# Window attention's key and query norms: an inverse root by a power on GpSimd in place of ScalarE's logarithm and exponential and VectorE's Newton step

## What is computed

```python
qkv = shift_token(x) @ wqkv                 # q, k, v: 8 heads of 64
q, k = l2norm(q) * q_scale, l2norm(k) * k_scale     # l2norm(t) = t / max(norm(t), 1e-12)
q, k = rotary_xpos(q, k)
sim  = 8 * q @ k.T                          # window of 128 and the one before it, masked
o    = softmax(sim) @ v
x    = x + o @ wo
h    = layernorm(shift_token(x)) @ w1 + b1  # a, g = halves of it
x    = x + (a * gelu(g)) @ w2 + b2
```

## Time and profile before

| | us |
|---|---|
| median of three runs (lowest, highest) | 1368.27 (1363.14, 1372.32) |
| the profiled execution, its own time | 1366.47 |
| its span, first to last instruction | 1364.7 |
| busy: TensorE (PE), VectorE (DVE) | 1241.3, 970.3 |
| busy: ScalarE (ACT), GpSimd (POOL) | 923.6, 634.0 |
| granted TensorE clock, mean over the span | 0.968 |

### The profile page before, as it was taken

One profiled execution on the slowest core, in us unless ns is written; L12 is line 12 of the kernel. 1 busy time (PEld: TensorE's weight loads), 2 busy tenths in 40 slices (PEclk: granted clock), 3 DMA queues, 4 the chain that ended last, 5 costly groups with the idle time before them and its releaser, 6 DMA issues.

```text
span 1364.7 us, 26379 instructions
## 1 busy us (share of the span) xinstructions
PE 1241.3 (91%) x9057; PEld 1061.2 (78%) x9057; DVE 970.3 (71%) x2602; ACT 923.6 (68%) x2023; POOL 634.0 (46%) x697
## 2 busy tenths in 40 slices
PE   2799999999999993899966988999999999999986
PEld 2699889989988993677754657888888887888886
DVE  5767666666767646998776787678788778777532
ACT  2455765565576552888936769778778788888643
POOL 6523521452353214444333556556656657655433
PEclk9799999999999997999987999999999999999999
DMA  7300010010000004000010001100100000000010
GB/s 165 103 1 14 32 32 1 14 64 0 1 1 1 1 0 114 1 17 17 9 65 1 1 5 52 40 5 5 46 4 4 20 5 13 20 21 21 21 31 17
DMA packets 34881, 33.75 MB, mean 25 GB/s; under 512 B 11340, under 2 KB 31424, under 8 KB 34752
## 3 DMA queue, kind: packets, MB, share of 16 engines
q1 hardware_dynamic: 33856, 29.91, 7.1%
q0 software_dynamic: 768, 2.10, 0.9%
q10 hardware_dynamic: 128, 0.04, 0.0%
HBM read 25.75 MB, written 4.19 MB: 22 GB/s over the span
## 4 chain that ended last, share of the span: by engine, by line
PE 40%; ACT 8%; DVE 4%; issue 3%; POOL 3%; DMA 2%; SPq 1%; ACTq 0%; DVEq 0%; POOLq 0%
PE w_ring L1633 2%; PE w_ps_p L1663 2%; PE w_ring L1635 2%; PE w_ring L1634 2%; PE w_ring L1713 2%; PE a_ps L845 2%; PE w_ring L1714 2%; PE w_ring L1715 2%; PE w_ps_a L1681 2%; PE w_ring L1640 2%; DMA w_xs<-X 2%; PE w_ring L1725 2%; PE w_ps_d L1656 1%; PE w_ps_d L1653 1%; PE w_ring L1726 1%
## 5 line engine op out<-in xcount | busy, mean ns | idle before, releaser
L360 ACT ACTIVATE t_gf<-t_ps_f,t_fb_cur 128x512 f32<-128x512 f32 x128 | 87.9, 686 | 165.8 <-PE t_ps_f L280 164.2
L508 DVE TENSOR_TENSOR t_g_lo<-t_gf,t_g_hi 128x512 fp32r<-128x512 f32 x128 | 92.1, 721 | 81.5 <-ACT t_g_hi L362 80.5
L293 PE MATMUL t_ps_o<-t_w_hi,t_g_hi 128*128 128x256 f32 x512 | 145.8, 285 | 1.1 <-DVE t_g_lo L508 1.1
L295 PE MATMUL t_ps_o<-t_w_hi,t_g_lo 128*128 128x256 f32 x512 | 144.8, 283 | 0.0
L294 PE MATMUL t_ps_o<-t_w_lo,t_g_hi 128*128 128x256 f32 x512 | 144.8, 283 | 0.0
L1713 PE MATMUL w_ring<-w_nh,w_w_hi 128*128 128x256 f32 x384 | 113.3, 295 | 12.8 <-DVE w_gate L2241 6.2
L644 POOL TENSOR_TENSOR t_rs<-t_ve,t_neghalf 128x4 f32<-128x4 f32 x32 | 38.2, 1194 | 178.7 <-DVE t_ve L469 177.2
L2196 DVE COPY w_pt<-w_ps_p 128x384 f32<-128x384 f32 x128 | 70.5, 550 | 60.7 <-PE w_ps_p L1663 59.6
L278 PE MATMUL t_ps_f<-t_nh,t_w_hi 128*128 128x512 f32 x256 | 103.5, 404 | 6.9 <-DVE t_nl L607 3.6
L1714 PE MATMUL w_ring<-w_nh,w_w_lo 128*128 128x256 f32 x384 | 108.0, 281 | 0.0
L1715 PE MATMUL w_ring<-w_nl,w_w_hi 128*128 128x256 f32 x384 | 107.9, 281 | 0.0
(11 more groups left out here) (290 smaller groups left out, 4368.6 us busy)
## 6 DMA issues: line engine op xcount, KB each, us to landing
t_raw<-in_L_tok_w SPq DMA_DIRECT2D x8, 1024.0 KB
out<-X SPq DMA_DIRECT2D x14, 256.0 KB, 2.2
raw<-in_L_ffn_wqkv SPq DMA_DIRECT2D x2, 1536.0 KB, 6.8
raw<-in_L_ffn_w SPq DMA_DIRECT2D x4, 682.0 KB, 5.2
w_raw_o<-out SPq DMA_DIRECT2D x8, 256.0 KB, 3.0
w_xs<-X SPq DMA_DIRECT2D x16, 127.0 KB
w_raw<-in_L_ffn_w SPq DMA_DIRECT2D x2, 640.0 KB
t_raw_d<-in_L_tok_D SPq DMA_DIRECT2D x4, 256.0 KB
```

The lines of the kernel that those rows point to most:

```text
L293: pe.matmul(out, g_hi[:, j % 4, tok], w2_hi[:, j, :], start=(j == 0 and t % 2 == 0), stop=False, skip_group_check=True)
L295: mm = pe.matmul(out, g_lo[:, j % 4, tok], w2_hi[:, j, :], start=False, stop=(j == FC - 1 and t % 2 == 1), skip_group_check=True)
L360: act.activation(gf[:, j % 2, :], ps_f[:, j % 2, :], ACT.Gelu, bias=fb_cur[:, j:j + 1]).then_inc(pf_free, 1)
L508: dve.tensor_tensor(g_lo[:, j % 4, :], gf[:, j % 2, :], g_hi[:, j % 4, :].bitcast(F32), ALU.subtract).then_inc(g_split, 1)
```

## The change

ScalarE's `root` and VectorE's `inverse_root` are taken out with their calls, and so are their four tiles and four semaphores. GpSimd's `scale_k` now begins with one power: `rn = sc ** -0.5` on the tile of 128 x 2 x 8, after a wait for the clamp and, from the third unit on, for the softmax steps that read the older `rn` of the same place (VectorE had this wait before). A tile `nhalf` of the same size, holding -0.5, is set once by VectorE in `pads`.

```diff
--- before.py
+++ after.py
@@ -1378,12 +1378,9 @@
     al = sb("al", [P, DC, STOK], F32R)
     ss = sb("ss", [P, 2, H])
     sc = sb("sc", [P, ST, 2, H])
-    lg = sb("lg", [P, ST, 2, H])
-    y0 = sb("y0", [P, ST, 2, H])
-    ya = sb("ya", [P, ST, 2, H])
-    yb = sb("yb", [P, ST, 2, H])
+    nhalf = sb("nhalf", [P, 2, H])
     rn = sb("rn", [P, 2, ST, 2, H])
-    return raw_o, raw_2, ln_all, b1_all, b2_all, tab, neghalf, ident, mask, x0_st, x0_mv, x0_ve, x0_rs, xs, ah, al, ss, sc, lg, y0, ya, yb, rn
+    return raw_o, raw_2, ln_all, b1_all, b2_all, tab, neghalf, ident, mask, x0_st, x0_mv, x0_ve, x0_rs, xs, ah, al, ss, sc, nhalf, rn
 
 
 def window_phase(nc, sems, X, dram, out, raw, qkv, opening, done):
@@ -1422,7 +1419,7 @@
 
         raw_qkv = raw[:, :].rearrange("p (c n) -> p c n", c=DC)
         raw_1 = raw[:, :].rearrange("p (c u n) -> p c u n", c=DC, u=2)
-        raw_o, raw_2, ln_all, b1_all, b2_all, tab, neghalf, ident, mask, x0_st, x0_mv, x0_ve, x0_rs, xs, ah, al, ss, sc, lg, y0, ya, yb, rn = opening
+        raw_o, raw_2, ln_all, b1_all, b2_all, tab, neghalf, ident, mask, x0_st, x0_mv, x0_ve, x0_rs, xs, ah, al, ss, sc, nhalf, rn = opening
         scl = raw_2[:, 0:2, :].rearrange("p c n -> p (c n)").rearrange("p (i u x) -> p i u x", i=2, u=2)
         m1 = sb("m1", [P, ST, 2, INNER])
         m2 = sb("m2", [P, 2, INNER])
@@ -1466,7 +1463,7 @@
 
         names = ("h_out h_in_0 h_in_1 b2_added stored vec ident maskz mask pad padp fill raw_qkv raw_o raw_2 raw_1 hi_qkv hi_o hi_2 hi_1 "
                  "split_qkv split_o split_2 split_1 tab x0 x0_st x0_mv x0_ve x0_rs t1_full ah_done split1 q_full k_full v_full sq_0 sq_1 "
-                 "ss_0 ss_1 q_read k_read rota_0 rota_1 sc_done lg_done y0_done ya_done yb_done rn_done kscaled qs_full ks_full qt_done kt_done v_done "
+                 "ss_0 ss_1 q_read k_read rota_0 rota_1 sc_done rn_done kscaled qs_full ks_full qt_done kt_done v_done "
                  "d_full sm_done p_done ri scaled p_full pt_done pv_done ot_h ot_split y_full x_mid shifted_0 shifted_1 st mv ve rs nmr xn "
                  "t2_full nf_done split2 g_full gelu_done a_full gated h_hi h_split h_used xb x_out")
         S = {x: sem(x) for x in names.split()}
@@ -1941,13 +1938,6 @@
                     act.wait_ge(done["v_full"], 2 * NSQ)
                 act.activation(m2[:, i, :], ring[:, RB[b], :], ACT.Square).then_inc(S[f"sq_{i}"], 1)
 
-            def root(n, t):
-
-                act.wait_ge(S["sc_done"], 2 * n + t + 1)
-                act.activation(lg[:, t, :, :], sc[:, t, :, :], ACT.Ln).then_inc(S["lg_done"], 1)
-                act.wait_ge(S["lg_done"], 2 * n + t + 1)
-                act.activation(y0[:, t, :, :], lg[:, t, :, :], ACT.Exp, scale=-0.5).then_inc(S["y0_done"], 1)
-
             def turned(n, t, i, b):
                 act.wait_ge(S["ks_full" if i else "qs_full"], 2 * n + t + 1)
                 if n >= 2:
@@ -2059,8 +2049,6 @@
                 if real(c):
                     probabilities(H * c + 0)
                     probabilities(H * c + 1)
-                if real(b):
-                    root(b, 0)
                 if real(c):
                     probabilities(H * c + 2)
                     probabilities(H * c + 3)
@@ -2075,8 +2063,6 @@
                     hi_1(1, 1)
                 if h == 13:
                     hi_2(1)
-                if real(b):
-                    root(b, 1)
                 if h == 3:
                     hi_o(0)
                 if real(c):
@@ -2160,18 +2146,6 @@
                     dve.wait_ge(S[f"ss_{i}"], 2 * n + t + 1)
                 dve.tensor_scalar(sc[:, t, :, :], ss[:, :, :], 1e-24, None, ALU.max).then_inc(S["sc_done"], 1)
 
-            def inverse_root(n, t):
-
-                k = 2 * n + t
-                dve.wait_ge(S["y0_done"], k + 1)
-                dve.tensor_tensor(ya[:, t, :, :], y0[:, t, :, :], y0[:, t, :, :], ALU.mult).then_inc(S["ya_done"], 1)
-                dve.wait_ge(S["ya_done"], k + 1)
-                dve.scalar_tensor_tensor(yb[:, t, :, :], ya[:, t, :, :], -0.5, sc[:, t, :, :], ALU.mult, ALU.mult).then_inc(S["yb_done"], 1)
-                dve.wait_ge(S["yb_done"], k + 1)
-                if n >= 2:
-                    dve.wait_ge(S["sm_done"], H * (n - 1))
-                dve.scalar_tensor_tensor(rn[:, n % 2, t, :, :], yb[:, t, :, :], 1.5, y0[:, t, :, :], ALU.add, ALU.mult).then_inc(S["rn_done"], 1)
-
             def soft(k):
 
                 m, h = divmod(k, H)
@@ -2287,15 +2261,11 @@
                     clamp(b, 1)
                 if real(c):
                     turned_p(H * c + 1)
-                if real(b):
-                    inverse_root(b, 0)
                 if real(e):
                     norm_stats(e)
                 if real(f):
                     gated(f, 0, 1)
                     gated(f, 1, 1)
-                if real(b):
-                    inverse_root(b, 1)
                 if real(d):
                     output_lo(NU * d + 3)
                 if real(c):
@@ -2337,6 +2307,7 @@
 
             def pads():
 
+                dve.memset(nhalf[:, :, :], -0.5)
                 dve.memset(neghalf[:, :], -0.5).then_inc(S["padp"], 1)
                 dve.memset(b1_all[:, :, :, :], 0.0).then_inc(S["pad"], 1)
                 dve.memset(xs[0:1, :, :, :], 0.0)
@@ -2395,6 +2366,10 @@
                 pool.tensor_tensor(m1[:, t, i, :], m1[:, t, i, :], m2[:, i, :], ALU.add).then_inc(S[f"rota_{i}"], 1)
 
             def scale_k(n, t):
+                pool.wait_ge(S["sc_done"], 2 * n + t + 1)
+                if n >= 2:
+                    pool.wait_ge(S["sm_done"], H * (n - 1))
+                pool.tensor_tensor(rn[:, n % 2, t, :, :], sc[:, t, :, :], nhalf[:, :, :], ALU.pow).then_inc(S["rn_done"], 1)
                 pool.wait_ge(S["rota_1"], 2 * n + t + 1)
                 pool.wait_ge(S["rn_done"], 2 * n + t + 1)
                 mk = m1[:, t, 1, :].rearrange("p (h d) -> p h d", d=HD)
```

## The result

The changed kernel takes 1402.49 us (median of four runs, 1401.38 to 1407.36) against 1369.97 us of the kernel before in runs beside it: a ratio of 1.0263, 95% interval 1.0232 to 1.0294. That is 2.6% slower; 1390.0 with a range of 1370 to 1411 was predicted. The profiled execution took 1401.38 us with a span of 1399.7, 35.0 us longer than the 1364.7 of before.

What follows compares the result with a forecast made beforehand. TensorE was taken as the bound, saturated in ten of sixteen passes, losing time only where another engine hands it work late. Losses pass by pass summed to 23.5 us: 1366.5+23.5 = 1390.0 us, range 1370 to 1411.

Steps and rivals of the forecast that it cites:

- relief elsewhere: Work taken from ScalarE and VectorE lies mostly beside TensorE's; with nothing added it would bring 6 us in all.
- its 3.6: Pass 5: ScalarE freed of the second root feeds GpSimd's hidden_lo sooner; about 3.6 us gained if nothing were added.
- a cheap power: Rival: 16 columns on GpSimd cost about 1 us, the delay hides and the relief remains, 1360.5 us; 18%.
- ScalarE was no bound: Rival judged: ScalarE bounds passes 2 to 5, removing its work gives 22.7 us, 1344 us; 6%.
- The power's size: GpSimd's 128x16 power, extrapolated from 128x2 and 128x4 at 152.5 ns a column: 2.84 us.
- The dear and the cheap end: Bounds of the power's time: 4.05 us (rival of 1424 us, 9%) and 0.71 us if more columns cost nothing.
- The walk through pass 6: Two powers on GpSimd make the third pair's scaling 2.2 us late, past the slack; TensorE stands 1.0 us per pass.
- the 7.0 of the sum: Passes 6, 7, 9, 10, 11, 14 and 15 lose 1.0 us each.
- The special passes: Losses in us: pass 8 1.3, 12 3.4, 13 2.5, 16 2.7, 2 0.8, 3 3.0, 4 1.6, 5 1.2.
- Pass 13's term: VectorE's variance sum took 3.44 us during GpSimd's weight split; split and sum move 0.8, then the power: 2.5 us lost.
- Passes 3 and 4: Pass 3 loses 3.0 us through x0_root(3) behind the second power; pass 4 loses 1.6 net of 1.6 relief.
- The rival of an absorbing queue: Rival: GpSimd's queue absorbs more than seen, so no change that can be told, about 1368 us; 10%.

Runs made afterwards that it cites:

- the kernel with the unused power: The kernel before, its root kept, plus one unused 128x16 power on GpSimd ahead of each scaling of keys; 1398.7 us, ratio 1.023.
- the cheap kernel: The changed kernel with a multiplication by a small constant in place of each of the 32 powers; 1359.99 us, ratio 0.9945 to the kernel before.
- the one with the larger dose: The changed kernel with one more, unused 128x16 power on GpSimd ahead of tile 1's scaling of keys; 1467.15 us, ratio 1.0725 to the kernel before.

## Why the prediction was right, and where it was short

- *TensorE is the bound, relief elsewhere is worth about 6 us.* Right: with a cheap operation in the power's place the kernel takes 6.4 us less than before. Pass 5 gives its 3.6 (38.9 us for 42.5) and passes 3 and 4 together 1.3 of their 1.6, as worked out. That the total is so near is partly luck: in the profiled executions passes 0 to 14 are 10.6 us shorter, and the rest takes 3.7 more. The two rivals that ended under the kernel before failed on different grounds: a cheap power would have given the 1360.5 worked out (1360.0 was measured with one), but the power isn't cheap; and ScalarE was no bound, since 72.7 us less work there bought only 6.4.
- *The power's size.* 2.84 predicted, 2.91 measured, and 0.14 instead of 0.05 until the scaling sees the result: 3.05 for 2.89, twice a pass. The dear and the cheap end, 4.05 and 0.71, are out.
- *The walk through pass 6.* Right in place and size: a wait of 1.0 predicted, 0.95 found. The pass grew by 1.2, though, which is just 6.1 less 4.9: the profile's wait leaves out some 0.2 us at each of these places, found as longer busy time at full clock (36.60 and 36.83 us in pass 9), in the kernel with the unused power too (0.61 of wait, 37.4 instead of 36.6). Seven steady passes, counting pass 15: 1.4 us more than the 7.0 of the sum.
- *The special passes.* The places and their order of size were right, and the wait of pass 8 nearly: 3.27 against 1.88+1.3. In pass 3 TensorE's wait grew by 3.9 (from 2.88 to 6.76) where 3.0 was predicted. Pass 13's term rests in part on VectorE's row of 3.44 us; the changed kernel has no such row, its same operation takes 169 ns in the mean, and the pass lost 3.9 for the 2.5 all the same. The step that failed is the sum over the special passes, which priced a wait at its own length. It had no term for TensorE's clock, though the kernel before shows its fall behind the wait of pass 5. Passes 8, 12, 13 and 16 each have a stretch at a lower granted clock behind their wait that the kernel before doesn't have there, and one such stretch costs 1.4 to 1.6 us in the only pair of passes that differ in nothing else. In pass 8 the pass lost 1.6 more than predicted at a wait of nearly the predicted length.
- *Passes 3 and 4* were mis-sized too: 69.6 us where the kernel before takes 63.4 and the one with the cheap multiplication 62.1. So the relief is 1.3 us, near the 1.6 of the prediction, and the powers cost 7.5, for which 3.0 and 3.2 were put in. The whole shortfall is in pass 3: 4.4 us more against the cheap kernel (34.7 for 30.4), and 3.2 in pass 4 (34.9 for 31.7). In pass 3 `x0_root(3)` starts 10.2 us behind TensorE's turn of the inputs at 779.09 instead of 6.2 behind the one at 777.63, so it came 4.0 us later for the 3 predicted. TensorE's 2.30 us in pass 4 are followed by full clock.
- *The sum.* 23.5 predicted; 35.0 in the two profiled executions. Of the 35.0, 26.7 are TensorE's idle time, so the waits were undervalued by 3.2 us, 1.8 of it in passes 3 and 4. The other 8.3 are longer busy time, for which the sum had no term: 6.1 in passes 8, 12, 13 and from 15 on, most of it behind the waits that lowered the clock, 1.4 at full clock in passes 6, 7, 9, 10, 11 and 14, and 0.8 before pass 6.
- *The rival of an absorbing queue* failed: in pass 6 all the idle time ahead of the third pair was used up, 4.9 us of room against 6.1.

## What to carry to other kernels

An operation moved to a less busy engine costs by what is queued behind it there, not by that engine's load: the same 32 powers cost some 40 us, by comparison with a cheap operation, in front of work that the bound engine takes next, and 2 us in the queue's idle places, so look first for the waits of the receiving engine and put the operation into them. Several delays on one in-order queue add up until its next wait, and the room ahead of that wait pays for the first ones only: one of these powers was free in a steady pass, two were not. When a sum of waits is made for TensorE, add what the clock may take behind the longer ones.

## What the runs showed of the hardware

- The power on GpSimd is slow by its operation, not by its place: 224 ns for a 128x16 multiplication, 2911 ns for the 128x16 power, 1640 for 128x8, 1012 for 128x4 and 707 for 128x2, so by a line through the ends about 157 ns for each column and 390 fixed. The 128x16 one was the same in every place in GpSimd's order, between 2899 and 2913 ns in the mean. The program's first phase has 128x4 powers too, and they take more, 1079 to 1194 ns in the means of these kernels.
- TensorE's granted clock fell to its lower level behind waits of 2.37 us in nearly all steady passes of one kernel and stayed at full in a pass that was the same up to that point; in the kernel before it was at 0.55 behind a wait of 2.62 us, at 1.00 behind 1.88. One fall cost 1.4 to 1.6 us in that kernel, and 1.2 to 2.7 behind waits of 3.6 us in the one with the larger dose.
- The next instruction of GpSimd that waits for its own last result starts 0.14 us after that ends; one that doesn't wait starts at once.
